# Turning the first normalised tile by a transposing DMA, with a reordered fill and drain, in an attention and mixture-of-experts kernel

## The reference

```python
x = x + xattn(layernorm(x), ctx, Wq, Wkv_expand, Wout)   # 16 heads of 32, causal, 64 keys a batch
x = x + ffn(layernorm(x), router_w, wg, wu, wd, sg_w, ...)
# xattn: q = n @ Wq.T ; k, v from ctx ; softmax(q k / sqrt(32)) v ; @ Wout.T
# ffn:   logits = n @ router_w.T ; top 2 of 8 experts, weighted by their logits
#        y = silu(n @ wg[e]) * (n @ wu[e]) @ wd[e], plus one shared expert with biases
```

## Time and profile before

| | us |
|---|---|
| median of three runs | 804.76 |
| the profiled execution, its own time | 803.22 |
| its span, first to last instruction | 801.5 |
| PE busy | 759.7 |
| DVE busy | 581.1 |
| ACT busy | 457.4 |
| POOL busy | 433.1 |

### The profile page before, as it was taken

How to read it: one execution, slowest core, us unless ns; L and a number is a source line. 1 busy time by engine, 2 the same in 40 slices (tenths; PEclk the granted TensorE clock), 3 DMA queues, 4 the chain that set the end, 5 groups by cost and what they waited for, 6 DMA issues and landing times.

```text
span 801.5 us, 21942 instructions
## 1 busy us (share of the span) xinstructions
PE 759.7 (95%) x7246; PEld 520.0 (65%) x7246; DVE 581.1 (72%) x1190; ACT 457.4 (57%) x844; POOL 433.1 (54%) x562
## 2 busy tenths in 40 slices
PE   3888999999999999889999999999999999999995
PEld 1566888878887888778888874455555555554552
DVE  4899899989999999846788775555555565555553
ACT  1767889989898989775556433333333333333330
POOL 2425777777777777544110202665655556556553
PEclk9899999999999999999999999999999999999998
DMA  8225668787877767767855655889999989889992
GB/s 289 92 70 152 182 184 237 210 218 215 227 207 232 202 203 195 192 189 236 253 186 208 207 191 131 136 137 162 143 156 147 160 144 152 154 132 165 145 144 37
DMA packets 138318, 140.73 MB, mean 176 GB/s; under 512 B 87872, under 2 KB 88896, under 8 KB 137856
## 3 DMA queue, kind: packets, MB, share of 16 engines
q1 hardware_dynamic: 122336, 104.01, 49.0%
q0 software_dynamic: 15904, 35.70, 25.6%
HBM read 71.61 MB, written 52.31 MB: 155 GB/s over the span
## 4 chain that ended last, share of the span: by engine, by line
PE 70%; DMA 8%; issue 2%; DVE 1%; ACT 1%; POOL 1%; SPq 1%; POOLq 0%; DVEq 0%
PE psum L1405 41%; PE psum L1463 16%; PE psum L1396 7%; PE psum L1509 3%; DMA out<-w_q,tabs 2%; DMA hidT<-xn2p 2%; PE psum L1551 2%; DMA magnitudes<-emag 1%; DMA x_in<-normed_tokens,tabs 1%; DMA normed_turned<-xn2T 1%; DMA mag_rows<-magnitudes 1%; DMA xn2T<-xn2p 0%; DMA xn1T<-normed_turned 0%; DVE w_q L1385 0%; POOL kv_store L608 0%
## 5 line engine op out<-in xcount | busy, mean ns | idle before, releaser
L726 POOL DMA_INDIRECT out<-w_q,tabs x71 | 112.7, 1587 | 108.6 <-DVE w_q L1385 72.6
L716 POOL DMA_INDIRECT x_in<-normed_tokens,tabs x71 | 71.0, 1000 | 89.9 <-DVE tabs L1266 42.2
L905 ACT ACTIVATE silu_g<-psum,tabs 128x256 f32<-128x256 f32 x71 | 33.6, 473 | 146.2 <-PE psum L1405 146.2
L1370 DVE SCALAR_TENSOR_TENSOR hid<-psum,tabs,silu_g 128x256 f32<-128x256 f32 x71 | 34.4, 484 | 111.5 <-ACT silu_g L905 111.5
L1405 PE MATMUL psum<-exp_all,hidT 128*128 x426 | 103.4, 379 | 1.2 <-DMA hidT<-xn2p 1.2
L1405 PE MATMUL psum<-exp_all,probsT 128*128 x420 | 96.4, 379 | 0.0
L1463 PE MATMUL psum<-xn1T,w_q 128*128 128x128 f16 x1536 | 91.0, 219 | 0.9 <-DVE w_q L954 0.9
L1405 PE MATMUL psum<-w_o,attnT 128*128 128x512 f16 x384 | 88.0, 379 | 0.0
L1463 PEld LDWEIGHTS psum<-xn1T,w_q 128*128 128x128 f16 x1536 | 86.3, 98 | 2.6 <-issue 2.4
L579 POOL TENSOR_TENSOR exp_all<-piece,exp_all 128x512 f32 (+1 forms) x48 | 56.0, 1168 | 47.7 <-ACT piece L746 47.7
L1405 PEld LDWEIGHTS psum<-exp_all,hidT 128*128 128x128 f16 x426 | 41.6, 98 | 51.8 <-issue 3.3
(11 more groups left out here) (211 smaller groups left out, 1671.8 us busy)
## 6 DMA issues: line engine op xcount, KB each, us to landing
x_in<-x SPq DMA_DIRECT2D x64, 256.0 KB, 3.0
exp_all<-experts SPq DMA_DIRECT2D x24, 512.0 KB, 5.2
out<-xy SPq DMA_DIRECT2D x32, 256.0 KB, 3.2
normed_tokens<-xn SPq DMA_DIRECT2D x32, 256.0 KB, 5.4
normed_turned<-xn2T SPq DMA_DIRECT2D x32, 256.0 KB, 3.5
w_q<-out SPq DMA_DIRECT2D x32, 256.0 KB, 3.3
out<-w_q SPq DMA_DIRECT2D x32, 256.0 KB, 2.5
probsT<-normed_turned SPq DMA_DIRECT2D x16, 256.0 KB, 3.5
```

Of the source, the lines that this page charges most:

```text
L716: pool.indirect_dma_start(x_in[:, t % 4, :], None, xn_dram, bass.IndirectOffsetOnAxis(gather_at[:, t:t + 1], 0)).then_inc(gathered[t % 4], 16)
L726: pool.indirect_dma_start(out, bass.IndirectOffsetOnAxis(add_at[:, t:t + 1], 0), y[:, t % Y_RING, :], None, bounds_check=TOKENS - 1, oob_i ...
L905: act.activation(silu_g[:, :], psum[:, GU_BANK[m % 2], 0:I], ACT.Silu, scale=gate_scale_at[:, tm:tm + 1]).then_inc(silu_ready, 1)
L1370: dve.scalar_tensor_tensor(hid[:, :], psum[:, GU_BANK[m % 2], I:2 * I], up_scale_at[:, tm:tm + 1], silu_g[:, :], ALU.mult, ALU.mult).then_ ...
```

## The change

The first normalised tile is treated like the second. ACT's normalisation now carries the factor 2^11, ACT copies it to fp16 (`xn1p[:, j % 2, 0]`), POOL subtracts for the low part at the end of its step, and SP turns both parts by one transposing DMA, one step later. `xn1p` has two buffers, which lie in the memory of `hidT`. PE's four transposes, ACT's copy out of bank 7 and DVE's low half go away.

```diff
@@ SP
+            def turn_first(tile, j):
+                sp.wait_ge(xn1_parts, tile + 1)
+                plain(sp)
+                wait(sp, q_mm, tile)
+                plain(sp)
+                sp.dma_start_transpose(xn1T[:, :, :, :].rearrange("p v c q -> p (v c) q"),
+                                       xn1p[:, j % 2, :, :].rearrange("p v h -> p (v h)")).then_inc(xn1_turned, 16)
...
                     sp.dma_start(out[bass.ds(t5 * P, P), :], base).then_inc(base_stored, 16)
+                if live(t1) and not (isinstance(t1, int) and t1 == 0):
+                    turn_first(t1, j + 1)
...
             load_x(0, 0)
+            sp.dma_start(wq_raw, wqT).then_inc(wq_in, 16)
             sp.dma_start(wk_sb, wkT).then_inc(ctx_in, 16)
...
-            sp.dma_start(wq_raw, wqT).then_inc(wq_in, 16)
             load_x(1, 1)
+            turn_first(0, 0)
+            sp.dma_start(r_raw, routerT).then_inc(wo_in, 16)
             sp.dma_start(wo_raw, woT).then_inc(wo_in, 16)
@@ POOL, the end of step
                 if len(pieces) > 1:
                     low_piece(e, pieces[1])
+                if live(tile):
+                    pool.wait_ge(xn1_hi, tile + 1)
+                    plain(pool)
+                    pool.tensor_tensor(xn1p[:, j % 2, 1, :], xn1[:, :], xn1p[:, j % 2, 0, :], ALU.subtract).then_inc(xn1_parts, 1)
@@ ACT, step
-                if live(t1) and not (isinstance(t1, int) and t1 == 0):
-                    turn_first(t1)
...
                     act.wait_ge(ln_rstd[0], tile + 1)
+                    wait(act, xn1_parts, tile)
                     act.activation(xn1[:, :], x_in[:, j % 2, 0:H], ACT.Identity, bias=rstd[:, 0, 2:3],
                                    scale=rstd[:, 0, 1:2]).then_inc(xn1_ready, 1)
+                    act.wait_ge(xn1_ready, tile + 1)
+                    wait(act, xn1_turned, 16 * (tile - 1))
+                    copy(xn1p[:, j % 2, 0, :], xn1[:, :], 1.0, xn1_hi)
@@ PE, step
-                    pe.wait_ge(xn1T_ready, t2 + 1)
+                    pe.wait_ge(xn1_turned, 16 * (t2 + 1))
...
+                entry_amid(tile, entry)
                 if live(t4):
...
-                if live(t1) and not (isinstance(t1, int) and t1 == 0):
-                    turn_first(t1)
...
-                entry_amid(tile, entry)
```

```diff
@@ ACT, first_weights
-                act.wait_ge(scales_ready, 1)
+                act.wait_ge(wo_in, 32)
+                row_sums(M_WO, wo_raw)
+                act.wait_ge(sums_ready, 1)
+                row_sums(M_R, r_raw)
+                act.wait_ge(wq_scale_ready, 1)
                 for half in range(2):
@@ DVE, first_weights
-                dve.wait_ge(wo_in, 32)
-                magnitude(M_WO, wo_raw)
-                magnitude(M_R, r_raw)
-                turn_first(0)
```

More of the change, by code:

```diff
@@ L564, in inv_std @@
                 plain(pool)
-                pool.tensor_scalar(rstd[:, which, 0:1], moments[:, which, 1:2], EPS, (1.0, X_UP ** -2)[which], ALU.add,
+                pool.tensor_scalar(rstd[:, which, 0:1], moments[:, which, 1:2], EPS, X_UP ** -2, ALU.add,
                                    ALU.mult).then_inc(ln_eps[which], 1)
@@ L590, in more_weights @@
                     batch_values(0)
-                if tile in (2, 3):
-                    for k in range(2 * tile - 4, 2 * tile - 2):
+                if tile == 3:
+                    for k in range(4):
                         pool.wait_ge(wo_scaled, 2 * (k + 1))
@@ L778, in more_weights, with last_weights @@
                         weight_piece(w_sh, sh_raw, k * PIECE, PIECE, M_GU if k < GU // PIECE else M_DOWN, wsh_scaled)
-            def turn_first(tile):
-                act.wait_ge(xn1T_mm, tile + 1)
-                copy(flat(xn1T[:, 0, :, :]), bank(7), X_UP, xn1T_hi)
+            def last_weights():
+                for k in range(2, 4):
+                    weight_piece(w_o, wo_raw, k * PIECE, PIECE, M_WO, wo_scaled)
+                weight_piece(w_r, r_raw, 0, C * E, M_R, wsh_scaled)
             def expert_sums(e, n):
@@ L791, in expert_sums @@
                 plain(act)
-                act.activation(sums_out, exp_raw[:, bass.ds(e * WE + start, size)], (ACT.Square, ACT.Square, ACT.Abs)[n],
+                out_here = sums_out
+                if isinstance(e, int) and e == E - 1:
+                    act.wait_ge(xn1_turned, 16 * T)
+                    out_here = xn1p[:, 1, :, :].rearrange("p n w -> p (n w)")
+                act.activation(out_here, exp_raw[:, bass.ds(e * WE + start, size)], (ACT.Square, ACT.Square, ACT.Abs)[n],
                                accum_out=emag[:, n:n + 1]).then_inc(e_mags, 1)
@@ L855, in step @@
                 if isinstance(t3, int) and t3 == 0:
-                    high_values(3)
+                    last_weights()
+                if isinstance(tile, int) and tile == 4:
+                    act.wait_ge(wsh_in, 16)
+                    row_sums(M_DOWN, sh_raw[:, GU:WE], sums_out)
                 if measured is not None and j == 2:
@@ L1443, in first_products @@
                 last.then_inc(k_mm, 1)
-                turn_magnitudes(1)
-                spread_magnitudes(1)
+                turn_magnitudes(2)
                 pe.wait_ge(scales_ready, 1)
                 values(0)
-            def turn_first(tile):
-                if isinstance(tile, int) and tile == 1:
-                    pe.wait_ge(v_split, 2)
-                pe.wait_ge(xn1_ready, tile + 1)
-                wait(pe, xn1T_ready, tile)
-                transposes(bank(7), xn1[:, :], C, xn1T_mm)
             pe.wait_ge(const_ready, 4)
```

112 lines of the change are left out of this document (64 added, 48 removed).

## The result

The changed kernel takes 845.72 us (median; 843.89 to 848.22), the one before 804.5 beside it on the same chip: 1.052 times as long, 95% interval 1.0488 to 1.0551. The direction was right, the size was not: +41 us where +25 was forecast, and 846 lies above the range's 841. The profiled execution's own time is 845.96 us, its span 844.1, 42.6 over the span before.

A forecast was written before the change was run, and what follows sets the result against it. PE bounds the tiles at 9.49 us a step, the POOL/ACT loop 0.46 us under it and lengthened past it by the change. Tiles +30, fill -4, drain -1 give +25 us: 829 us, range 812 to 841.

The forecast's parts named there:

- parts 2, 3: POOL/ACT loop: copy adds 0.79 us, subtract 1.12, so 10.94 a step with pieces, 10.25 without; +30.0 over all tiles.
- part 4: Transposing DMA on SP: turned tile lands 3.4 us (2.0 to 5.7) after the subtract; cost taken as nothing.
- part 6: Drain: PE's waits get the shared product in front of them; -1 us, between -4 and +3.
- What bounds it: Tiles: PE sets 9.49 us a step; the loop over POOL and ACT takes 9.03, only 0.46 under it.
- Part 1: PE loses four transposes, 0.47 us a step; DVE 0.68 a tile; counted as nothing where the loop is longer.
- The +22 kept as the other end of that term: Transposing DMA's upper case: +1 us in each of 22 steps, beside the zero taken.
- That the clock falls then, I don't expect: PE, idle about 1.9 us a step in the tiles, was expected to keep its granted clock.
- Part 5: Fill: DVE loses work, first split and query product move forward 1 to 3 us; -4 us, between 0 and -10.
- Loop and turn both late: Rival: turned tile lands 5.7 us after issue, PE's product 1 us late in 22 tiles; 851 us, chance 0.07.
- PE stays the bound: Rival: the subtracts fit POOL's idle time, PE's 0.47 us partly return; 785 to 793 us, chance 0.09.
- About even: Rival: copy hides in ACT's idle time, fill wins near its bound; 806 to 811 us, chance 0.09.
- The signs: Right: spacing 10.9 us, ACT waiting 1.5, PE waiting for `qT`, 83 to 85% busy. Wrong: PE's wait ended by the DMA.

The follow-up runs named there:

- 7: Kernel before with only the new fill: PE still turns the first tile, old drain order; 797.9 us, ratio 0.9902.
- 9: 7 plus ACT's copy and POOL's subtract in their places, results unread, no transposing DMA of the first tile; 827.0 us.
- 12: run 9 plus SP's transposing DMA of their result at the changed kernel's place, into memory nobody reads; PE still turns the tile; 833.1 us.
- 13: Changed kernel with PE's shared product put back behind the transposes of attention and probabilities in the drain; 845.2 us, ratio 1.0510.
- 15: Same kernel as 13 (changed kernel, old drain order), measured again; 843.6 us, ratio 1.0471.
- 14: Changed kernel unaltered, measured again; 847.7 us, ratio 1.0545.
- run 4: Changed kernel with ACT's copy behind its first high piece and the subtract given to DVE at its step's end; 838.6 us, ratio 1.0438.
- run 10: 7 plus one same-size transposing DMA a step in tiles 11 to 32, for which nobody waits; 805.5 us, ratio 1.0029.
- 1: Changed kernel with its fill and drain, but PE turns the first tile again; new copy, subtract and transposing DMA removed; 801.9 us, ratio 0.9964.
- 5: run 4 with SP's turn issued one step earlier, ahead of the logits' store; 825.1 us, ratio 1.0239.
- 2: Changed kernel with POOL's new subtract moved ahead of the first low piece; 837.4 us, ratio 1.0410.
- 3: Changed kernel with ACT's new copy moved behind its first high piece; 839.6 us, ratio 1.0424.

## Why the forecast was right in direction and wrong in size

The sum, by the ratios, taken times 804 us; for the changed kernel with either drain the mean of its two runs stands. What a step is worth depends on what was there before it, so the table holds in this order only:

| step | from runs | measured | forecast |
|---|---|---|---|
| new fill | 7 | -7.9 | -4 |
| copy and subtract in the loop (parts 2, 3) | 9 less 7 | +31.8 | +30 |
| the turn, unread (part 4) | 12 less 9 | +4.8 | 0 |
| PE's wait for the turned tile (part 4) | 13, 15 less 12 | +10.6 | 0 |
| the drain's order (part 6) | changed, 14 less 13, 15 | +3.4 | -1 |
| sum | | +42.8 | +25 |

- **What bounds it, and parts 2 and 3: right.** The loop from `inv_std(0)` over `xn1`, the piece and `inv_std(1)` was the limit 0.46 us away, its terms held to 0.2 us, and its +30 came out as +31.8, with nothing else changed. Some luck is in how near that is: in the profiles runs 9 and 7 differ by 26.8 us between the first `inv_std` of tiles 7 and 31, where the terms give 28.5, and by 2.3 ahead of tile 7, which the terms left out. The average, POOL at 54% to 55% of its span, shows nothing of it.
- **Part 1: counted as nothing, and nothing of it was seen.** Its 0.47 us is the row of the weight loads; the products of the same four transposes take 0.60 us in the same step (PE, 209.13).
- **Part 4: the step that failed.** "I take nothing", since there were "nearly 2 us of idle time to cover a late one": the landing was read as 2.0 to 5.7 us, and the median of 3.4 set against PE's wish "some 3 us into that step". The runs showed 4.8 us for the turn itself and 10.6 for PE's wait for it, 15.4 in place of 0. Two things were left out. The turn's start is tied to the end of POOL's step on one side and to the end of the query product on the other, because `xn1T` has one buffer, so its late end is a loop of its own: with the POOL loop open (run 4) it still holds a batch at 41.1 us. And one more turn a step makes the other turn land late as well (run 10). Of the 10.6 us, runs 13 and 15 less 12, the profiles have 7.7 in tiles 12 to 30, all of it in steps without pieces, and 3.3 ahead of tile 7. The +22 kept as the other end of that term would have covered it; the range did not take it in whole.
- **"That the clock falls then, I don't expect": right for the idle time it spoke of, wrong with a late turn.** In runs 9 and 12, with steps of the forecast's length, the granted clock is 1.00 over tiles 12 to 30. In the changed kernel it is 0.97: three products behind waits of 4.41, 2.28 and 2.12 us took 5.30, 4.46 and 4.48 us for 2.84, 5.7 us more, and the three steps behind them are the long ones.
- **Part 5: direction and place right, size too small for the fill by itself, too large in the changed kernel.** Tile 7 begins 4.5 and 6.6 us sooner in runs 7 and 1, which share a fill. With copy and subtract (run 9) 2.2 are left, and 1.0 in the changed kernel; in runs 13, 14 and 15, with the same fill, tile 7 begins at 86.1, 85.8 and 84.4 us. Part 5 did not count what copy, subtract and turn cost in the first tiles.
- **Part 6: wrong sign.** Not the first shared product's wait was the matter, but what is queued behind it on PE's list: the transposes of `attn` and `probs`, ready before, stand behind 3.48 us of waiting and a product of 4.47 us, at a granted clock of 0.63.
- **The rivals.** "Loop and turn both late", 851 us at 0.07, had the mechanism that happened, though not its place (1 us in each of 22 steps there, a few steps without pieces and the fill here), and lies 5 us from the result; it deserved much more, since its only condition was the upper half of a spread that I had quoted. "PE stays the bound" fell: the steps are 10.8 us. "About even" fell: the copy isn't hidden.
- **The signs.** Spacing 10.9, ACT's wait of 1.4 us on average before `xn1` and PE's wait for `qT` came as listed under right; PE's wait ended by the transposing DMA came too, which I had listed under wrong, as if only one of the two could be. PE is busy for 87% of tiles 12 to 31, over the 83 to 85 given.

On the rule: the Trainium skill, DMA: Bandwidth & Descriptors, section Rules for kernel authors, says to issue a transfer early, compute, and wait for it late. The runs agree: the same turn issued sooner on SP's list is worth 13.4 us (run 4 to 5).

Open: why runs 2 and 3 gave so nearly the same time, how the late turn's cost divides between wait and clock, what the unread turn delays after tile 31, and what a second buffer for `xn1T` would give, which wasn't tried.

## What to carry to other kernels

When work moves from an engine to a DMA, draw the DMA's loop as well: what must end before it may be issued, where it stands in its issuer's list, when it lands at the slow end of the spread, and which single-buffered tile closes the circle. Two loops of nearly equal length hide each other (opening the POOL loop alone gave back 7 of 41 us), so price each by itself, with the other left out and its results unread. And a change with several parts is worth taking apart even when it loses: the new fill alone takes 1% less time than the kernel before.

## What the hardware did that I had not expected

The turn, 128 x 1024 in fp16, landed after 2.8 to 6.3 us, the longest beside an expert's load and the other turn, whose issue itself then took 1.99 us on SP for the usual 1.24; the weight loads of PE's four fp32 transposes of the tile took 0.47 us. After a wait of 4.41 us PE's granted clock was 0.50 for the whole product that followed, 5.30 us for 2.84, and products behind waits of 2.28 and 2.12 us took 4.46 and 4.48 us. And a turn that nobody reads still costs 7.6 us in 22 steps at a DMA share of 0.93 (run 10).
